# Last expert stage of a four-layer kernel: second-layer weights through ScalarE into fixed tiles, and VectorE's work of a pair in another order

## What is computed

```python
hn2 = _layernorm(x, ln2_g, ln2_b).reshape(-1, h)      # 4096 tokens x 128
logits = hn2 @ gate_w + gate_b                        # 8 experts
idx = jnp.argmax(logits, axis=-1)                     # one expert a token
mid = jax.nn.relu(jnp.einsum('th,ehf->etf', hn2, w1) + b1[:, None, :])   # 128 -> 512
y = jnp.einsum('etf,efh->eth', mid, w2) + b2[:, None, :]                 # 512 -> 128
moe = y[idx, jnp.arange(hn2.shape[0])]
return x + moe.reshape(b, s, h)
```

## Time and profile before

| | |
|---|---|
| Median of 3 runs | 1835.48 us (1835.18 to 1840.15) |
| The profiled execution | 1857.31 us, its span 1854.6 us |
| Mean granted TensorE clock | 0.79 of full speed |
| PE / PE weight load / DVE / ACT / POOL busy | 69% / 46% / 66% / 40% / 50% |
| First layer of the first pair of the last stage starts | 1715.29 us into the span |
| Last scatter issued | 1842.66 us, taking 0.97 us |

### The profile page before, as it was taken

How to read it: one execution, slowest core, us unless ns; L and a number is a source line. 1 busy time by engine, 2 the same in 40 slices (tenths; PEclk the granted TensorE clock), 3 DMA queues, 4 the chain that set the end, 5 groups by cost and what they waited for, 6 DMA issues and landing times.

```text
span 1854.6 us, 27625 instructions
## 1 busy us (share of the span) xinstructions
PE 1273.5 (69%) x8554; PEld 857.2 (46%) x8555; DVE 1229.5 (66%) x2820; ACT 740.7 (40%) x1207; POOL 926.3 (50%) x996
## 2 busy tenths in 40 slices
PE   2434332548888887878788887568778777783775
PEld 1222221425666666656566667523333333331665
DVE  6778771157788887777777784266777677663443
ACT  1101100335455554455445544145555555552322
POOL 2355566546666666666666644321332313223663
PEclk8555555568888888888988886669988898986988
DMA  4000002600000000000000000030000000000110
GB/s 130 25 16 26 14 2 52 132 12 2 7 8 8 7 6 3 3 6 6 6 6 6 7 4 4 16 104 13 18 10 17 9 17 17 9 12 21 60 58 13
DMA packets 73493, 41.41 MB, mean 22 GB/s; under 512 B 23825, under 2 KB 68729, under 8 KB 73424
## 3 DMA queue, kind: packets, MB, share of 16 engines
q1 hardware_dynamic: 53040, 28.88, 5.6%
q0 software_dynamic: 20384, 11.67, 3.1%
HBM read 31.63 MB, written 23.87 MB: 30 GB/s over the span
## 4 chain that ended last, share of the span: by engine, by line
PE 40%; DVE 33%; issue 10%; ACT 6%; POOL 5%; DMA 2%; another core or an unknown queue 1%; POOLq 1%; DVEq 0%; SPq 0%; ACTq 0%
PE psum L1111 8%; PE psum L1162 5%; PE psum L1216 4%; DVE terms L1731 4%; DVE o L1573 4%; PE psum L1345 2%; PE psum L1358 2%; POOL o_inv L634 2%; PE psum L1139 2%; PE psum L1239 2%; PE psum L1249 2%; PE psum L1277 2%; PE psum L1120 1%; DVE rden L1425 1%; POOL xe_dram L573 1%
## 5 line engine op out<-in xcount | busy, mean ns | idle before, releaser
L1111 PE MATMUL psum<-v,attn 128*128 128x64 f32 x2048 | 288.5, 301 | 25.7 <-ACT aggr L845 17.1
L1111 PEld LDWEIGHTS psum<-v,attn 128*128 128x128 f32 x2048 | 272.7, 214 | 61.6 <-issue 44.9
L1731 DVE TENSOR_REDUCE terms<-psum 128x2 bf16<-128x512 f32 x256 | 165.5, 690 | 37.2 <-PE psum L1239 28.5
L609 POOL DMA_INDIRECT yg<-ye_dram,routel x128 | 139.2, 1088 | 65.5 <-issue 36.0
L695 POOL TENSOR_SCALAR veps<-meanvar 128x2 f32<-128x2 f32 x32 | 6.1, 191 | 330.9 <-DVE meanvar L1709 329.8
L573 POOL DMA_INDIRECT xe_dram<-rows_out,route x128 | 131.1, 1024 | 39.6 <-issue 38.7
L1216 PE MATMUL psum<-prob,v 128*32 128x256 f32 x1024 | 148.8, 415 | 1.1 <-ACT pvT L919 0.8
L914 ACT ACTIVATE prob<-psum 128x512 f32<-128x512 f32 x256 | 138.5, 597 | 18.8 <-PE psum L1204 18.8
L830 ACT ACTIVATE attn<-psum 128x1024 f32<-128x1024 f32 x128 | 129.9, 1015 | 11.9 <-PE psum L1094 10.7
L1120 PE MATMUL psum<-ident,o 128*128 128x128 f32 x256 | 48.5, 351 | 102.3 <-DVE o L1573 78.9
L1239 PE MATMUL psum<-k_highT,q_highT 32*128 32x256 bf16 x512 | 56.6, 303 | 76.9 <-DVE terms L1731 73.0
(11 more groups left out here) (297 smaller groups left out, 2975.8 us busy)
## 6 DMA issues: line engine op xcount, KB each, us to landing
x4n_dram<-x4n SPq DMA_DIRECT2D x16, 256.0 KB
w<-in_w POOLq DMA_DIRECT2D x48, 64.0 KB, 2.5
x_in<-in_x SPq DMA_DIRECT2D x8, 256.0 KB, 2.8
xe_dram<-zero_rows SPq DMA_DIRECT2D x8, 256.0 KB, 3.5
x_dram<-x1s SPq DMA_DIRECT2D x8, 256.0 KB
xe_dram<-rows_out,route POOLq DMA_INDIRECT x128
xe<-xe_dram SPq DMA_DIRECT2D x16, 128.0 KB
x1l<-x_dram SPq DMA_DIRECT2D x16, 128.0 KB, 2.2
```

Of the source, the lines that this page charges most:

```text
L609: pool.indirect_dma_start(yg[p][:, j, k, :], None, ye_dram, bass.IndirectOffsetOnAxis(ap=where[:, j, K0 + k:K0 + k + 1], axis=0), bounds_c ...
L1111: mm = pe.matmul(psum[:, 4 + j, (head % HALF) * DV:(head % HALF + 1) * DV], attn[g % RING][:, h, c * SEQ + j * P:c * SEQ + (j + 1) * P], v ...
L1731: dve.tensor_reduce(terms4[:, 0, j, head:head + 2, 6, 0], bank[4 + a2].rearrange("q (b k) -> q b k", b=2), AX, ALU.max, negate=True).then_ ...
```

## The change

ScalarE gets four new tiles, `wb_now` (two sets of two), and copies the second-layer weights of the next pair's two experts into them (`place_second`), one value load before each copy, after the wait that the pair before the current one has left PE. ScalarE's two value loads for the biases move to the head of the pair, and its first turn is written out. PE loses its two value loads; its second layer reads `wb_now` at fixed addresses and waits for `wb_made`. VectorE loads both numbers at the head of the pair, does both blocks' rectifiers first, then places both blocks' first-layer weights, then both residuals.

```diff
+        wb_now = [two(f"wb_now{n}_", [P, CHUNKS * D]) for n in range(2)]
...
+            def place_second(pair, h, p):
+                expert = act.value_load(block_expert_i[0:1, bass.ds(2 * pair + p, 1)], min_val=0, max_val=E1 - 1)
+                act.activation(wb_now[h % 2][p][:], wb[:, bass.ds(expert * CHUNKS, CHUNKS), :].rearrange("q c d -> q (c d)"), ACT.Copy).then_inc(s["wb_made"], 1)
+
             def turn(i, last=False):
                 for h in range(AHEAD // 2):
                     pair = AHEAD // 2 * i + h
+                    expert = [act.value_load(block_expert_i[0:1, bass.ds(2 * pair + p, 1)], min_val=0, max_val=E1 - 1) for p in range(2)]
                     for p in range(2):
-                        expert = act.value_load(block_expert_i[0:1, bass.ds(2 * pair + p, 1)], min_val=0, max_val=E1 - 1)
                         act.wait_ge(s["mid_ps"], 4 * pair + 2 * p + 1)
                         for c in range(2):
-                            ins = act.activation(mid[p][:, c, :], bank[4 * p + 1][:, c * P:(c + 1) * P], ACT.Relu, bias=ba[:, bass.ds(expert * CHUNKS + c, 1)])
+                            ins = act.activation(mid[p][:, c, :], bank[4 * p + 1][:, c * P:(c + 1) * P], ACT.Relu, bias=ba[:, bass.ds(expert[p] * CHUNKS + c, 1)])
                         ins.then_inc(s["mid_act"], 1)
                     if not last or h < AHEAD // 2 - 1:
                         for p in range(2):
                             turned(pair + 1, p)
+                        wait(act, s["res_ps"], 2 * pair)
+                        for p in range(2):
+                            place_second(pair + 1, h + 1, p)
 
             for p in range(2):
                 turned(0, p)
-            with act.Fori(0, BLOCKS // AHEAD - 1) as i:
+            for p in range(2):
+                place_second(0, 0, p)
+            turn(0)
+            with act.Fori(1, BLOCKS // AHEAD - 1) as i:
                 turn(i)
             turn(BLOCKS // AHEAD - 1, last=True)
...
             def turn(i, last=False):
                 for h in range(AHEAD // 2):
                     pair = AHEAD // 2 * i + h
-                    expert = [pe.value_load(block_expert_i[0:1, bass.ds(2 * pair + p, 1)], min_val=0, max_val=E1 - 1) for p in range(2)]
...
                     for p in range(2):
                         pe.wait_ge(s["mid_act"], 2 * pair + p + 1)
                         pe.wait_ge(s["mid_dve"], 2 * pair + p + 1)
+                        pe.wait_ge(s["wb_made"], 2 * pair + p + 1)
                         wait(pe, s["res_made"], 2 * pair)
                         for c in range(CHUNKS):
-                            mm = pe.matmul(bank[4 * p + 3][:, 0:D], mid[p][:, c, :], wb[:, bass.ds(expert[p] * CHUNKS + c, 1), :].rearrange("q c d -> q (c d)"), start=(c == 0), stop=(c == CHUNKS - 1))
+                            mm = pe.matmul(bank[4 * p + 3][:, 0:D], mid[p][:, c, :], wb_now[h % 2][p][:, c * D:(c + 1) * D], start=(c == 0), stop=(c == CHUNKS - 1))
                         mm.then_inc(s["res_ps"], 1)
...
             def turn(i, last=False):
                 for h in range(AHEAD // 2):
                     pair = AHEAD // 2 * i + h
+                    expert = [dve.value_load(block_expert_i[0:1, bass.ds(2 * pair + p, 1)], min_val=0, max_val=E1 - 1) for p in range(2)]
                     for p in range(2):
-                        expert = dve.value_load(block_expert_i[0:1, bass.ds(2 * pair + p, 1)], min_val=0, max_val=E1 - 1)
                         dve.wait_ge(s["mid_ps"], 4 * pair + 2 * p + 2)
                         for c in (2, 3):
-                            ins = dve.tensor_scalar(mid[p][:, c, :], bank[4 * p + 2][:, (c - 2) * P:(c - 1) * P], ba[:, bass.ds(expert * CHUNKS + c, 1)], 0.0, ALU.add, ALU.max)
+                            ins = dve.tensor_scalar(mid[p][:, c, :], bank[4 * p + 2][:, (c - 2) * P:(c - 1) * P], ba[:, bass.ds(expert[p] * CHUNKS + c, 1)], 0.0, ALU.add, ALU.max)
                         ins.then_inc(s["mid_dve"], 1)
+                    if not last or h < AHEAD // 2 - 1:
+                        for p in range(2):
+                            place_weights(pair + 1, p)
+                    for p in range(2):
                         q = 2 * h + p
                         wait(dve, s["res_sent"][q], 16 * i)
-                        dve.tensor_tensor(res[q][:], got[q][:, 0:D], bb[:, bass.ds(expert * D, D)], ALU.add).then_inc(s["base_made"], 1)
-                        if not last or h < AHEAD // 2 - 1:
-                            place_weights(pair + 1, p)
+                        dve.tensor_tensor(res[q][:], got[q][:, 0:D], bb[:, bass.ds(expert[p] * D, D)], ALU.add).then_inc(s["base_made"], 1)
```

More of the change, by code:

```diff
@@ L420, in build_program @@
             s[name] = [sem(f"{name}{n}") for n in range(AHEAD)]
-        for name in ("all_counted count_ps plan_made experts_in tokens_landed tokens_out tokens_ps rows_made wa_made base_made g5T_ps g5T_made mid_ps mid_act mid_dve res_ps res_made").split():
+        for name in ("all_counted count_ps plan_made experts_in tokens_landed tokens_out tokens_ps rows_made wa_made wb_made base_made g5T_ps g5T_made mid_ps mid_act mid_dve res_ps res_made").split():
             s[name] = sem(name)
```

## The result

| | before | after |
|---|---|---|
| median of 4 runs each | 1837.82 us | 1816.12 us |
| range | 1835.18 to 1840.95 us | 1809.46 to 1818.86 us |
| ratio after / before | | 0.9876, 95% interval 0.9843 to 0.9909 |
| second session (before 7 runs, after 4) | 1836.00 us | 1812.00 us, ratio 0.9859 (0.9842 to 0.9875) |
| the last expert stage, profiled | 129.97 us | 103.25 us (second profile 102.12 us) |

What follows compares the result with a forecast made beforehand. GpSimd's DMA issues were taken to become the bound, at 5.39 us a pair: stage 26.4 us shorter, less 3.2 us for the low clock, gain 23.2 us; from the median 1835.48 this gives 1812.3 us, range 1807 to 1825.

Steps and rivals of the forecast that it cites:

- The two gaps: PE idle in a loop pair: 1.17 us between second layers (VectorE's late rectifiers), 1.06 us between pairs (PE's value loads).
- GpSimd as the next bound: In the last expert stage GpSimd's DMA issues become the longest round; a pair goes from 6.62 to 5.39 us.
- rival 2: GpSimd's issues held up by VectorE's copies: round 6.25 us, 13.8 us worse than forecast, 1826 us; chance 0.08.
- The low clock: Four half-clock stretches in the loop cost PE 0.8 us each, 3.2 us in all, taken off the gain.
- The rounds of the other engines: Own work per loop pair: VectorE 5.2 us, ScalarE 5.1 us, PE 4.43 us, against GpSimd's 5.39 us.
- Rival 1: Value loads on ScalarE or VectorE become the bound: loop pair 5.8 to 5.9 us, 1822 us; chance 0.17.
- Rival 3: PE's gaps stay because `wa_now` copies come 1 us later than reckoned: 1835 us again; chance 0.08.
- Rival 4: The low clock takes over on PE: stage ends 8 us later, 1843; chance 0.05 with anything else that costs.

Runs made afterwards that it cites:

- each part alone: VectorE's new order alone, in the kernel before: 1809.15 us; ScalarE's placement and PE's fixed addresses alone, the changed kernel with VectorE's old order: 1808.09 us.
- the kernel with the order alone: The kernel before with only VectorE's new order (both rectifiers, both weight copies, both residuals), PE keeping its value loads: stage 106.64 us, median 1809.15 us, ratio 0.9886.

## Why the prediction was right, step by step

*The two gaps.* Right in their causes. The gap between the second layers was VectorE's late rectifiers and the gap between pairs was PE's value loads: each part alone closes its gap and leaves the other. At the start of the stage PE's first layer now begins 0.26 us after the second transpose starts (1703.27), against 1.63 us: 1.4 us gained where 1.1 was forecast.

*GpSimd as the next bound.* Right, in place and in size. From the first scatter to the end the sum had 86.2 us for sixteen pairs and 10.2 after that, 96.4; the profile has 85.9 and 10.4, from 1709.98 to 1806.26, 96.28 us. The rows of the issues moved little:

```profile
L758 POOL DMA_INDIRECT out<-res,rows_of x40 | 41.1, 1028 | 13.1 <-issue 11.3 <-DVE res L1909 1.8
...
L752 POOL DMA_INDIRECT got<-x4n_dram,rows_of x37 | 38.3, 1035 | 11.3 <-issue 11.3
```

1028 and 1035 ns against 1019 and 1030, so rival 2, every issue held up by VectorE's copies, is out: less than 0.01 us an issue. Its mechanism is there all the same, in single issues. Of the 77 issues in this stage, read from the timelines of GpSimd and VectorE, 44 that meet no weight copy take 1.01 us on average and at most 1.02; 16 begin while one runs and take 1.11 on average, up to 1.23 us, and all eleven of 1.08 us or more are among them. In the stage before, nine began inside a copy. By the Trainium skill (SBUF — State Buffer, SBUF: two separate sides) such a copy takes a GpSimd DMA from 620 to 3100 ns; the trace agrees that an issue inside a copy is held up, and has 0.2 us where that has 2.5.

*The low clock.* Wrong. The sum took off 0.8 us for each of four stretches at 1.2 GHz, 3.2 us. In both profiles of the changed kernel there was none from the second pair on; the undiminished 26.4 us was the stage's real gain (26.7 and 27.9). That the whole-kernel gain, 21.7 to 24.0 us, is nearer to the diminished 23.2 is no credit to that term: medians of four runs that spread over 4 to 9 us don't tell 23 from 26. That the forecast gain lies so near the measured one is in part luck.

*The rounds of the other engines.* All three were sized too high, on the side that did no harm. VectorE was 5.2 us in the forecast and is 4.55 in the kernel with half the scatters. ScalarE was 5.1; with copies 1.8 us a pair longer, pairs of 4.56 us still occur, with ScalarE busy all the time, so in the kernel as it is it needs less than that, its loads hidden behind its queued work. PE was 4.43 by its busy time and is 3.80: the busy time of a group that runs into a gap contains the last matmul's length, 0.28 us, where a group that is followed by another contributes only its spacing, (1.95 - 0.28) / 15 = 0.11 us; 34 passes at that spacing are 3.8 us. Rival 1 (value loads bound, 1822) rested on these sizes; had GpSimd's round been 4.5 instead of 5.4 us it would have been VectorE's loads that bound the kernel, and at 4.55, not at 5.85.

*What the prediction didn't say.* That each part alone would do. It was in its own numbers: with GpSimd at 5.39 us and PE's pair at 6.62, 1.2 us of the gaps' 2.2 was all that could be had, and each gap alone was 1.1. The prediction summed the whole change against the bound and never asked it of the parts.

*The other rivals.* Rival 3 (the gaps stay, because `wa_now` comes late) is wrong: the changed kernel's profile has no wait of PE for `wa_now`, and the 11.6 us that carry its name in the kernel with the order alone are PE's value loads. Rival 4 went the other way: no low-clock stretch in either profile after the first pair.

## What to carry to other kernels

Where two changes each remove a stall from the same chain, work out the round of every engine and queue that isn't yet the bound, DMA issues with the pauses between them included; the next one up caps the sum of both, and either alone may reach the cap. Further work on this stage pays only in fewer indirect DMA issues: ScalarE, VectorE and PE have room of 0.8 us a pair and more. In these kernels a value load cost what the queue ahead of it couldn't cover: nothing beside long copies on ScalarE, about a microsecond for two at the head of a pair on VectorE or PE. And when the label of a wait on several semaphores decides something, look at when each of the engines waited for was done: it was wrong twice here.

## What the runs showed of the hardware that I had not expected

**Low-clock stretches in the long stages, next to none in the short ones.** With the stage at 129 to 130 us, in the kernel before with all and with half of its scatters, the granted clock falls to 0.5 (1.2 GHz) four and five times in the loop, for some 3.4 us each, and the stage's mean is 0.92 and 0.90. In the ten profiles whose stage is 87 to 107 us it is 0.97 to 0.99, and in nine of them 1.00 once the first pair is over. One, all scatters with ScalarE's loads shared, has a single stretch, with a clock of 0.57 in each of the two stretches of 2 us from 1788 to 1792. In the 4 us before it PE had worked 1.22 and 1.15 of 2 us, and it had worked as little elsewhere in the same stage without a fall (0.73 of 2 us from 1764.00). The stages differ in PE's gaps, but what decides when the clock falls was not tested.

**An indirect DMA issue keeps its mean price when the engines beside it get busier.** 1.01 to 1.05 us on average with 0.30 between two, in every kernel here, from the stage of 130 us to that of 87; single ones take up to 1.25 us. In the changed kernel the long ones begin inside one of VectorE's weight copies.
